# New order at both ends of a local-attention pipeline, split transposes, one normalisation moved to ScalarE, idle products removed

## What is computed

```python
x = x + L0_xattn(layernorm(x), ctx)       # 16 heads of 64
x = x + L0_ffn(layernorm(x))              # 6 times: local attention (qkv, rotary, Wo) and a GEGLU ffn
x = x + L1_xattn(layernorm(x), ctx)       # 16 heads of 8
x = x + L1_ffn(layernorm(x))              # a linear layer with fp8 inputs
x = x + L2_xattn(layernorm(x), ctx)       # 16 heads of 8
x = x + L2_ffn(layernorm(x))              # shared expert and 8 routed experts, all evaluated and gated
x = x + L3_xattn(layernorm(x), ctx)       # 16 heads of 8
x = x + L3_ffn(layernorm(x))              # 8 experts, gated by similarity
```

## Time and profile before

| | us |
|---|---|
| median of 3 runs | 2427.15 |
| lowest and highest | 2426.22, 2431.37 |
| profiled execution, its own time | 2429.43 |
| its span | 2427.6 |
| TensorE busy | 2350.2 (97%) |
| VectorE (DVE) busy | 1884.5 (78%) |
| ScalarE (ACT) busy | 1487.6 (61%) |
| GpSimd (POOL) busy | 1195.7 (49%) |

### The profile page before, as it was taken

One profiled execution on the slowest core, in us unless ns is written; L12 is line 12 of the kernel. 1 busy time (PEld: TensorE's weight loads), 2 busy tenths in 40 slices (PEclk: granted clock), 3 DMA queues, 4 the chain that ended last, 5 costly groups with the idle time before them and its releaser, 6 DMA issues.

```text
span 2427.6 us, 60848 instructions
## 1 busy us (share of the span) xinstructions
PE 2350.2 (97%) x25488; PEld 1423.9 (59%) x25488; DVE 1884.5 (78%) x3376; ACT 1487.6 (61%) x2142; POOL 1195.7 (49%) x932
## 2 busy tenths in 40 slices
PE   7998999999999999999999999988899999999998
PEld 6785666666666666666666666645555555455443
DVE  6889899999999999999999989957866766445222
ACT  3344666666666666666666666643476777566443
POOL 2336777777777777777777777721211111101000
PEclk9999999999999999999999999988999999999999
DMA  3000000000000000000000100002010100120110
GB/s 127 9 8 6 2 2 28 10 8 7 28 11 8 7 28 11 13 2 28 11 13 3 35 2 11 2 4 87 10 41 6 41 33 15 55 85 30 36 43 22
DMA packets 36183, 56.29 MB, mean 23 GB/s; under 512 B 6397, under 2 KB 20869, under 8 KB 35657
## 3 DMA queue, kind: packets, MB, share of 16 engines
q1 hardware_dynamic: 35912, 52.40, 6.8%
HBM read 51.19 MB, written 1.19 MB: 22 GB/s over the span
## 4 chain that ended last, share of the span: by engine, by line
PE 72%; DVE 19%; ACT 4%; issue 3%; POOL 1%; DVEq 0%; POOLq 0%; ACTq 0%
PE w L1607 9%; PE w L1597 9%; PE w L676 6%; PE w L657 6%; PE w L667 5%; DVE turned L1147 4%; PE w L427 4%; PE py L697 4%; PE w L721 3%; PE w L750 3%; DVE norm L1154 2%; PE w L731 2%; PE pt L780 2%; PE py L784 2%; PE w L1690 2%
## 5 line engine op out<-in xcount | busy, mean ns | idle before, releaser
L438 ACT ACTIVATE prob<-logit 128x512 f32<-128x512 f32 x224 | 137.7, 631 | 285.2 <-DVE logit L446 285.2
L1597 PE MATMUL w<-qT,m_fc 128*128 128x512 f32 x544 | 267.6, 604 | 0.4 <-ACT turned L1856 0.4
L1332 POOL TENSOR_TENSOR straight_odd<-straight_odd,turned 128x1024 f32<-128x1024 f32 x96 | 226.7, 2371 | 65.5 <-DVE turned L1147 65.5
L468 POOL TENSOR_TENSOR prob<-prob,rden 128x1024 f32<-128x1024 f32 x112 | 213.8, 1909 | 90.2 <-DVE rden L457 90.2
L1147 DVE TENSOR_TENSOR turned<-w,rot 128x512 f32<-128x512 f32 x384 | 245.5, 681 | 0.0
L1332 POOL TENSOR_TENSOR straight<-straight,turned 128x1024 f32<-128x1024 f32 x96 | 226.7, 2372 | 36.1 <-DVE turned L1147 36.1
L1326 POOL TENSOR_TENSOR straight_odd<-straight_odd,rnorms 128x1024 f32<-128x1024 f32 x96 | 180.7, 1903 | 118.2 <-DVE rnorms L1168 118.2
L1154 DVE TENSOR_REDUCE norm<-sq 128x16 f32<-128x1024 f32 x192 | 224.2, 1209 | 0.0
L487 POOL TENSOR_TENSOR fresh_roots<-fresh_means,eps 128x1 f32<-128x1 f32 x64 | 12.3, 192 | 393.0 <-DVE fresh_means L475 393.0
L1326 POOL TENSOR_TENSOR straight<-straight,rnorms 128x1024 f32<-128x1024 f32 x96 | 180.7, 1903 | 43.0 <-DVE rnorms L1168 43.0
L676 PE MATMUL w<-b_wqkv,m_proj 128*128 128x512 f32 x384 | 190.4, 618 | 2.1 <-DVE logit L446 2.1
(11 more groups left out here) (285 smaller groups left out, 5332.6 us busy)
## 6 DMA issues: line engine op xcount, KB each, us to landing
b_wqkv<-gates SPq DMA_DIRECT2D x64, 256.0 KB, 3.7
b_wqkv<-in_b_wqkv SPq DMA_DIRECT2D x18, 512.0 KB, 3.6
ctxT<-in_ctxT SPq DMA_DIRECT2D x64, 64.0 KB, 1.8
b_wo<-in_b_wo SPq DMA_DIRECT2D x6, 512.0 KB, 3.7
m_fc<-in_m_fc SPq DMA_DIRECT2D x1, 2304.0 KB, 8.8
m_proj<-in_m_proj SPq DMA_DIRECT2D x1, 2304.0 KB, 12.8
m_fc<-in_m_fc SPq DMA_DIRECT2D x8, 256.0 KB, 3.8
m_proj<-in_m_proj SPq DMA_DIRECT2D x8, 256.0 KB, 3.7
```

What stands on the lines that cost most here:

```text
L468: pool.tensor_tensor(flat, flat, k.rden[:, s, :, None].broadcast_to([P, HEADS, SEQ]), ALU.mult).then_inc(k.prob_ready, 1)
L1332: pool.tensor_tensor(k.straights[s][:, i, :, :], k.straights[s][:, i, :, :], k.turned[:, i, :, :], ALU.add).then_inc(added, 1)
L1597: pe.matmul(claim(("hidden", J, c)), k.m_fc[:, x, c * P:(c + 1) * P], k.m_xT[:, q, :], start=True, stop=True).then_inc(k.ring_full, 1)
```

## The change

It has four parts.

1. **Start.** The 71 increments now go to TensorE and ScalarE alone. Eight 128x128 products of the identity with itself, into a bank that is overwritten later, stand ahead of the first transpose. In the first step the transpose and the copy of the second tile go ahead of the keys; in the third step (`g == 2 - TILES`) the scores go ahead of the transposes of the probabilities.
2. **End of the local pipeline.** TensorE, ScalarE and DVE get a new order in `end_of_layers` and `in_slot`; `in_slot` now has two places in a slot on TensorE (behind the scores, and at the end) and two on ScalarE. `turn_out(1)` uses the other banks, and scores wait for fewer add-backs.
3. **Front slots.** `turn_probs` is cut into 4 transposes, `rows`, and the other 4. The idle products are gone.
4. **Row normalisation.** The write of `y_all` for all 48 works goes from DVE to ScalarE, as `x * root + (0 - mean * root)`, one slot later; GpSimd makes the factor `below` with two more 128x1 operations for each work.

```diff
@@ start @@
-            for s, first in primed[0::4]:
+            for s, first in primed[0::2]:
                 pe.sem_inc(s, first)
...
+    for i in range(8):
+        pe.matmul(k.w2[:, 0:P], k.ident[:, :], k.ident[:, :], start=True, stop=True)
     turn_x(-TILES)
...
+        if g == -TILES:
+            turn_x(g + 1)
         if is_cross(g):
             cross_keys(g)
...
-        if before2:
+        if before2 and g != 2 - TILES:
             turn_probs(g - 2, before)
...
+        if g == 2 - TILES:
+            turn_probs(g - 2, before)
@@ end of the pipeline, TensorE @@
-    w = k.w0 if q == QUADS - 1 else k.w1
+    w = (k.w1, k.w1, k.w0, k.w0)[q]
...
         quad_turn(LAST - 1)
-        turn_out(0)
+        turn_probs(STEPS - 1, False)
         end_hidden(LAST - 1, 0)
-        turn_probs(STEPS - 1, False)
-        end_hidden(LAST - 1, 1)
         pe.wait_ge(k.pT_ready, FIRST + STEPS)
         attend_tensor(pe, k, (STEPS - 1) % 2, k.w2).then_inc(k.o_psum, 1)
-        turn_out(1)
-        end_hidden(LAST - 1, 2)
+        turn_out(0)
+        end_hidden(LAST - 1, 1)
         rows(STEPS // 2 - 1, STEPS + 2)
         rows_end(STEPS // 2 - 1)
-        end_output(LAST - 1)
+        end_hidden(LAST - 1, 2)
         end_in()
...
+        if (u, place) == (0, "end"):
+            end_output(LAST - 1)
+            turn_out(1)
+        if (u, place) == (1, "scores"):
             end_turn()
-        if u == 1:
+        if (u, place) == (1, "end"):
             for c in range(3):
                 end_hidden(LAST, c)
-        if u == 2:
             end_output(LAST)
-        if u == 3:
+        if (u, place) == (2, "end"):
+            turn_out(2)
+        if (u, place) == (3, "end"):
             turn_out(3)
@@ end of the pipeline, DVE @@
         fed(LAST - 2, k.py)
+        gate(LAST - 1, 0)
         add_back(0)
         first_stats(0)
-        gate(LAST - 1, 0)
+        dve.wait_ge(k.o_psum, FIRST + STEPS)
+        dve.memset(k.end.hid[64:P, 2, :], 1.0)
         first_normalise()
         first_stats(1)
         gate(LAST - 1, 1)
-        dve.wait_ge(k.o_psum, FIRST + STEPS)
-        dve.memset(k.end.hid[64:P, 2, :], 1.0)
-        add_back(1)
-        gate(LAST - 1, 2)
         dve.wait_ge(k.row_psum, p + 1)
         feed(k.py, 4 * p % (2 * TILES), 4).then_inc(k.row_added, 1)
         quad_stats(LAST)
-        fed(LAST - 1, k.end.lines)
+        gate(LAST - 1, 2)
...
         if u == 0:
-            add_back(2)
+            fed(LAST - 1, k.end.lines)
+            add_back(1)
         if u == 1:
             for c in range(3):
                 gate(LAST, c)
+            fed(LAST, k.end.lines)
         if u == 2:
-            fed(LAST, k.end.lines)
+            add_back(2)
@@ front slots @@
         else:
-            pe.wait_ge(k.back_added, QUADS - 1)
+            pe.wait_ge(k.back_added, 2)
...
-        layers_in_slot(u)
-        if u > END_SLOTS:
-            occupy()
-            occupy()
+        layers_in_slot(u, "end")
         if before2:
             turn_rows(before2[2], u)
         if before:
-            turn_probs(before[2])
+            turn_pairs(before[2], range(PAIRS // 2))
         if before2:
             rows(before2[0], before2[2], u)
+        if before:
+            turn_pairs(before[2], range(PAIRS // 2, PAIRS)).then_inc(d.pT_psum, 1)
@@ row normalisation @@
+    def fresh_normalise(t, W):
+        n, s = k.fresh, W % 2
+        act.wait_ge(n.lowered, W + 1)
+        act.activation(k.y[:, t, :], k.x[:, t, :], ACT.Identity, bias=n.below[:, s, :],
+                       scale=n.roots[:, s, :]).then_inc(n.normed, 1)
...
         if work:
             turned_x(work[2])
+        if work_at(u - 3):
+            fresh_normalise(*work_at(u - 3)[1:])
         if job:
             gelu(job, 1)
...
+    def fresh_gpsimd(W):
+        n, s = k.fresh, W % 2
+        pool.wait_ge(n.normed, PHANTOM + W + TILES - 1)
+        rstd_gpsimd(pool, k, n, PHANTOM + W + TILES, s)
+        pool.wait_ge(n.rstd, PHANTOM + W + TILES + 1)
+        pool.tensor_tensor(n.below[:, s, :], n.means[:, s, 0:1], n.roots[:, s, :], ALU.mult).then_inc(n.scaled, 1)
+        pool.wait_ge(n.scaled, W + 1)
+        pool.tensor_tensor(n.below[:, s, :], k.zero4[:, 0:1], n.below[:, s, :], ALU.subtract).then_inc(n.lowered, 1)
```

More of the change, by code:

```diff
@@ L73, in build @@
         k.fresh.roots = sb("fresh_roots", [P, 2, 1])
+        k.fresh.below = sb("fresh_below", [P, 2, 1])
         k.normed = sb("normed", [P, 2, P])
@@ L255, in build @@
         k.fresh.normed = sem("fresh_normed", PHANTOM)
+        k.fresh.scaled = sem("fresh_scaled")
+        k.fresh.lowered = sem("fresh_lowered")
         B = PHANTOM + TILES
@@ L375, in _ @@
         def _(act):
-            for s, first in primed[1::4]:
+            for s, first in primed[1::2]:
                 act.sem_inc(s, first)
@@ L385, in _ @@
         def _(pool):
-            gpsimd_program(nc, pool, k, primed[2::4] + primed[3::4])
+            gpsimd_program(nc, pool, k)
 def wait_apart(eng, k, s, value):
@@ L804, in turn_out @@
             pe.wait_ge(k.shifted, FIRST + STEPS)
-        elif q < QUADS - 1:
+        elif q == 2:
+            pe.wait_ge(k.z_fed, ALL_QUADS)
+        else:
             pe.wait_ge(k.back_added, q)
@@ L911, in layers_tensor @@
             rows(p, g)
-        if is_cross(g + 1) and g >= -TILES:
+        if is_cross(g + 1) and g > -TILES:
             turn_x(g + 1)
@@ L997, in end_of_layers, with in_slot @@
         unshift(0)
+        turned_probs(g)
         gelu(LAST - 1, 0)
-        turned_probs(g)
+        outputs(g)
         gelu(LAST - 1, 1)
-        outputs(g)
         unshift(1)
         gelu(LAST - 1, 2)
-    def in_slot(u, work):
-        if u == 0 and not work:
+    def in_slot(u, place):
+        if (u, place) == (0, "front"):
+            quad_normalise(LAST)
+        if (u, place) == (1, "turned x"):
+            affine(LAST)
             unshift(2)
-        if u == 0 and work:
-            quad_normalise(LAST)
-            affine(LAST)
-        if u == 1 and work:
+        if (u, place) == (1, "front"):
             for c in range(3):
@@ L1015, in in_slot @@
             act.preload_act_table_set("natural_log_exp_and_others")
-        if u == 3 and not work:
+        if (u, place) == (2, "front"):
             unshift(3)
@@ L1046, in layers_scalar @@
             act.copy(k.v2[:, 1 - s, :, :], k.w2[:, :]).then_inc(k.v_ready, 1)
+        if g == -TILES:
+            turned_x(g + 1)
         if is_cross(g):
@@ L1049, in layers_scalar @@
             act.copy(k.kT[:, s, :, :], k.w1[:, :]).then_inc(k.kT_ready, 1)
-        if is_cross(g + 1):
+        if is_cross(g + 1) and g > -TILES:
             turned_x(g + 1)
@@ L1730, in rows, with turn_pairs, turn_probs @@
         pe.matmul(k.py[:, P:2 * P], k.s_oT[:, :], k.s_w[:, n, 3, :], start=True, stop=True).then_inc(d.y_psum, 1)
-    def turn_probs(W):
+    def turn_pairs(W, pairs):
         w = logits_bank(k, W)
         pe.wait_ge(d.exp, PHANTOM + W + 1)
-        for h in range(PAIRS):
+        for h in pairs:
             mm = pe.transpose(w[:, h * P:(h + 1) * P],
                               k.prob[:, W % 2, 2 * h:2 * h + 2, :].rearrange("p a m -> p (a m)"), k.ident[:, :])
-        mm.then_inc(d.pT_psum, 1)
-    def occupy():
-        if claimed:
-            pe.wait_ge(k.ring_read, claimed[-1] + 1)
-        pe.matmul(k.w2[:, 512:1024], k.ident[:, :], k.s_w[:, 0, :, :].rearrange("p a n -> p (a n)"),
-                  start=True, stop=True)
+        return mm
+    def turn_probs(W):
+        turn_pairs(W, range(PAIRS)).then_inc(d.pT_psum, 1)
     def front_slot(u, work, before, before2):
@@ L1751, in front_slot @@
             scores(before[2])
+        layers_in_slot(u, "scores")
         if work:
@@ L1920, in merged_scalar @@
             gelu(job, 3)
-        layers_in_slot(u, False)
+        layers_in_slot(u, "turned x")
         if work:
             front(work[0], work[2])
-        layers_in_slot(u, True)
+        layers_in_slot(u, "front")
         if u < LEAD:
@@ L2132, in merged_vector @@
             normalise(after[1], after[2])
-        before3 = work_at(u - 3)
-        if before3 and u <= LEAD:
-            fresh_normalise(before3[1], before3[2])
         if before2 and u < LEAD:
@@ L2148, in merged_vector @@
             gates(*GATES_AT[u])
-        if before2 and u >= LEAD:
-            fresh_normalise(before2[1], before2[2])
         layers_in_slot(u)
@@ L2186, in merged_gpsimd @@
         if before2:
[L2187 removed]
+            fresh_gpsimd(before2[2])
         if u == SIM_AT - 1:
@@ L2355, in gpsimd_program @@
     pool.tensor_copy(k.ident16[:, :], k.ident[:, :]).then_inc(k.consts, 1)
-    for s, first in primed:
-        pool.sem_inc(s, first)
     layers_gpsimd(pool, k)
```

11 lines of the change are left out of this document (4 added, 7 removed).

## The result

| | before | changed |
|---|---|---|
| median | 2427.63 (4 runs) | 2442.82 (4 runs, 2442.01 to 2443.96) |
| profiled execution | 2429.43 | 2442.01 |
| its span | 2427.6 | 2440.2 |
| mean granted clock | 0.988 | 0.975 |

The account below looks back on a forecast made before the run. TensorE, busy 2350.2 of 2427.6 us, was taken as the bound, leaving its pauses and granted clock. Terms -3.2 - 8.0 - 1.1 - 2.7 + 10 - 2.5 = -7.5 gave 2420 us, range 2404 to 2438.

Parts of the forecast that it names:

- the clock without idle products, +10: Steady front slots: pauses left by the removed idle products lower TensorE's clock in part of them, 10 us slower.
- I take two slots in five at the low clock: Seven steady front slots: 0.4 of the 24.5 us that all at 1.2 GHz would cost, giving +10.
- slow front slots: Rival, chance 0.15: the clock falls in the first slot without idle products and stays low, +24.5; 2439 us in all.
- The clock holds: Rival, chance 0.28: front-slot pauses of 1.3 and 0.4 us don't matter and the ends give their full -9.9; 2408 us.
- No pause under 1.9 was followed by the low clock: Argument from the earlier trace for the rival (0.28) in which front-slot pauses of 1.3 and 0.4 us don't matter.
- Split turn, -2.7: Front slots: nothing in seven steady ones (up to +0.6), -1.3 in slot 4, -0.5 each in slots 7, 8, 11, 12.
- Start, -3.2: Kernel start: -1.25 from the earlier second transpose, -1.0 from increments and eight products, -1.0 from earlier scores.
- Ends, -8.0 and -1.1: Pipeline end: fewer waits and a higher clock give -8.0; idle products and add-back in slots 3 and 4 give -1.1.
- 0.7 lost between the shorter pieces: End of the local pipeline: about 0.7 us of new waits between the shorter pieces, counted against the gain.
- The ends give little: Rival, chance 0.12: slots 1 to 3 each wait 1.93 us for an add-back, so 5.8 of the gain goes; 2426 us.
- Normalisation, -2.5: Expert slots, last fp8 input: -1.2 from a shorter DVE wait, 1.3 more if the clock keeps; bounds 0 to -2.7.
- At nothing: Expert slots: the new ScalarE activation of about 0.3 us per tile was costed at no time.

Follow-up runs that it names:

- e1: The changed kernel with the two idle products put back into front slots 3 to 15: 2418.88 us, ratio 0.9957 to the kernel before.
- e2: The kernel before with only its idle products taken out: 2439.68 us, ratio 1.0046.
- e5: The changed kernel, still without idle products, with the turn of the probabilities in one piece: 2428.52 us, ratio 1.0000 to the kernel before.
- e4: The changed kernel with the idle products back and the turn of the probabilities in one piece again: 2413.81 us, ratio 0.9941 to the kernel before.
- e7: The kernel before with only the new order of the pipeline's end and of slots 0 to 3: 2424.04 us, ratio 0.9975.
- e8: The kernel before with the new ends and the row normalisation on ScalarE; idle products and whole turn kept: 2416.28 us, ratio 0.9950.
- e6: The kernel before with the new start and new ends; idle products, whole turn and normalisation on DVE kept: 2420.11 us, ratio 0.9970.
- e10: As e4, with the semaphore increments spread over the engines as before: 2416.32 us, ratio 0.9948 to the kernel before.
- e11: As e4, without the eight products ahead of the first transpose: 2415.69 us, ratio 0.9945 to the kernel before.
- e9: As e4, with idle products moved ahead of the transposes in the two fp8-input front slots and added to slot 2: 2411.49 us, ratio 0.9923.

## Why the prediction was wrong

**The term that failed is "the clock without idle products, +10"**: it is 25. "I take two slots in five at the low clock" was the step: the windows show 84% of the second half of the front slots there, and six of the seven steady slots were longer by 2 us or more. The price of a slot was near: these six are 3.35 us longer on average where I had 3.5. The mechanism was right, the idle products were removed from a pause and the clock fell, and e1 and e2 show it from both sides. But I costed the term as if the split turn, which I had put at nothing for the steady slots, had no part in it. With the whole turn it is 14 (e5 against e4) or 11 (e2), not far from 10; the other 11 us come only with the split turn. I had argued that a slow slot leaves TensorE busier and so brings the clock back. It does come back, but a slow slot also has its own pauses: ScalarE takes the exponentials behind the copies of the last products, and in slot 14 TensorE waits 0.98 us for the copy of the probabilities and 1.77 for the exponentials. The rival "slow front slots" had the right size, and I gave it 0.15. I had also read the earlier trace rows too simply: slot 15, "a little longer", takes 10.98 us in the kernel before, and lost the most, 5.8.

**"The clock holds" is refuted**, and so is the reading of the earlier trace rows as its proof: one pause of 1.42 us in a dense stretch does not tell what happens if it recurs. e2's three slots with 1.54 us at full clock show that even a few repetitions don't. "No pause under 1.9 was followed by the low clock" doesn't hold in slots 13 and 14 of e5, where none was over 1.33.

**Split turn, -2.7 in "front slots at full clock"**: not there. With the idle products e1 is 3.9 us above e4, within the noise; without them the split costs 15. Of its parts, -0.5 each for slots 7 and 11 came (-0.7), but slots 8 and 12 lost more than that. I let the row products "only change places" with four transposes and looked at the next transpose of x alone; the copy of the turned probabilities, which waits for the last transpose, was queued behind.

**Start, -3.2**: -2.9 in the profile, which was luck: almost all of it arises at the stop near 60 us, which e7 and e8 shorten with the old start. The eight products were mis-sized twice. I took "some 2 us on" as their start and 1.9 us as their length; but the 16 records of the earlier trace rows are eight products of the code, since each fp32 product shows as two, so that eight take 3.75. They started at 6.28 and held the first transpose until 9.82, 4 us later than before:

```profile
6.28 3.75 PE L889 MATMUL w<-ident 128*128 128x128 f32 x16 [6.28 <-issue]
...
9.82 0.42 PE L579 MATMUL pt<-ident,normed 128*128 128x128 f32 x1
...
10.64 2.11 PE L588 MATMUL w<-xT,m_fc 128*128 128x128 f32 x16 [0.40 <-issue]
```

The increments that I took off GpSimd, 0.71 us, cost TensorE 2.75. The stop at 60 us stood in the trace of before and I didn't look there. Over whole runs the start is -1.2 or -2.2, within the noise.

**Ends, -8.0 and -1.1**: -8.5 up to slot 3 in the profile, near -8.0, but not by the sum's terms. I had -6.2 from the waits and 0 to -3.7 from the clock; the waits gave -2.2 and the products 6.3 us less, by the clock. The wait of 1.93 behind turn_out(1) came at 1.78; the "0.7 lost between the shorter pieces" was too small, since six more waits of 0.3 to 1.2 stand there. Over whole runs the ends are -6.1 (e7) in place of -9.1. What is missing is slot 3, for which I had a gain: 8 of the 12 profiles with the new ends have it at the low clock, 11.4 to 12.8 us long in place of 8.2. "The ends give little" had about the right size for e7, but by that clock and not by its mechanism: only one new wait for an add-back came, 1.77 ahead of slot 1's scores. The other, ahead of slot 4's (1.93 in e7), stood there before.

**Normalisation, -2.5**: right in its place and sign, but too small: 3.5 us at the last fp8 input in e8's profile where I had 2.5, and -6 to -7 over runs, since it also shortens the front slots. "At nothing" for ScalarE held: TensorE's wait for its activations in the slots with experts is 0.4 us before and after.

**Slots with experts, -0.4 in the change**: the gain of -3.8 that e8 shows there is lost again because the low clock of the front slots reaches into the first of them (0.63 from 1765 to 1792, 0.94 before).

From kernel to kernel (before, e7, e6, e4, e1, changed) the ratios give ends -6.1, start -1.2, normalisation -7.0, split turn +3.9 and idle products +25.3. That they add up to the change's 15 proves nothing, since each kernel stands between the same two ends; and the last two are not separate prices, as e5 shows.

What stays open: why the same kernel, e5 for one, spreads over 16 us between runs, and what decides where the clock falls. That the stop of TensorE at 53 to 60 us is a fetch of instructions held up by the weights' loads is a guess; it wasn't tried. The loads run at 324 GB/s from 52 to 60 us in the kernel before and at 329 in the changed one, which has no stop, so the loads alone don't make it.

## What to carry to other kernels

Idle work on TensorE that looks free to remove, because it ends before the next product can start, may be what holds its clock; take out half of it first (one of two products held the clock here), and test it apart from any reordering. When costing a move, follow every consumer of the last instruction of the moved group, not only the next instruction on the same engine. Three parts that together gain 14 us here (e4) were hidden by one loss of 25: time the parts apart. And test two parts that touch the same pause together as well as apart: the missing idle products cost 14 us beside a whole turn and 25 beside a split one. A total that agrees with the profile doesn't confirm its terms; the ends' -8 came from the clock and hardly from the waits.

## What was not expected of the hardware

- Fp32 transposes hold the clock as products do: 14 idle transposes a slot (1.7 us) gave 2417.0 us, two idle products (1.9 us) 2418.9, neither of them 2442.8.
- Short pauses are enough to lose it: without idle products the longest pause in slots 13 and 14 of e5, where the clock fell, was 1.33 us, and yet e2 kept it through three slots with 1.54 each.
- Semaphore increments ahead of an engine's program aren't free: 18 more on TensorE moved its first product from 3.52 to 6.27 us, 0.15 each by that division.
- TensorE stopped for 1.5 to 3.4 us within a run of products (the kernel before, e2, e7, e8, e10, e11), with "issue" as the only cause; in the kernel before the clock fell after it. e10's lead of 2.2 us over e4 ahead of that place was gone behind it.
- The time of one kernel is uneven, and the granted clock goes with it: 2406.9 (0.994) to 2417.4 us (0.990) in e4, 2421.7 (0.985) to 2437.7 (0.975) in e5, 2409.5 to 2412.2 in e9.
